# A hand-ordered decoder layer: own instruction lists for the first steps, a ramp and the end, moments of x in groups, and h transposed as 32-bit words

## The reference

```python
def _layernorm(x, eps=1e-05):                       # mean and variance over the last axis
    return (x - m) / jnp.sqrt(v + eps)

x = x + self_attention(_layernorm(x))               # 16 heads of 8
    # attn = softmax(q k^T * 8**-0.5 + (rel_pe @ w_rel)[q - k]); out = attn v @ w_out + b_out
x = x + cross_attention(_layernorm(x), ctx, ctx, mask)
    # 16 heads of 8, scores = where(mask == 0, -1e9, scores)
x = x + ffn(_layernorm(x))                          # 128 -> 512 -> 128
    # act_quant: scale = 127 / max|x| of the row; round(x * scale) / scale
    # weights: round(w / mean|w|) clipped to -1, 0, 1, times mean|w|
    # gate = silu(q(x) @ w_gate); up = q(x) @ w_up; q(gate * up) @ w_down
```

## Time and profile before

| what | value |
|---|---|
| three runs | 458.35, 461.51, 463.34 us, median 461.51 |
| span of the profiled execution, first to last instruction | 457.5 us |
| busy over the span | PE 398.0 (87%), DVE 385.7 (84%), ACT 359.9 (79%), POOL 329.2 (72%) |

### The profile page before, as it was taken

One profiled execution on the slowest core, in us unless ns is written; L12 is line 12 of the kernel. 1 busy time (PEld: TensorE's weight loads), 2 busy tenths in 40 slices (PEclk: granted clock), 3 DMA queues, 4 the chain that ended last, 5 costly groups with the idle time before them and its releaser, 6 DMA issues. The chain is left out here.

```text
span 457.5 us, 18022 instructions
## 1 busy us (share of the span) xinstructions
PE 398.0 (87%) x5405; PEld 311.5 (68%) x5436; DVE 385.7 (84%) x1920; ACT 359.9 (79%) x962; POOL 329.2 (72%) x917
## 2 busy tenths in 40 slices
PE   3267879999999999999999999999999999877762
PEld 2245657777777777777877777778877777654430
DVE  4645467999999999999999999999999999888532
ACT  2214758899999999999999999999999998865542
POOL 6834667888888888888888888888888765654120
PEclk9998999999999999999999999999999999998655
DMA  6654577756666766676657675676567662422100
GB/s 190 162 146 100 140 188 184 173 149 172 173 159 160 191 163 168 150 195 172 170 148 196 175 175 153 164 181 170 152 158 189 165 164 80 101 78 77 30 6 13
DMA packets 100181, 67.27 MB, mean 147 GB/s; under 512 B 73269, under 2 KB 90421, under 8 KB 100085
## 3 DMA queue, kind: packets, MB, share of 16 engines
q1 hardware_dynamic: 98209, 64.08, 54.7%
q10 hardware_dynamic: 1876, 2.03, 1.5%
HBM read 46.08 MB, written 19.07 MB: 142 GB/s over the span
## 5 line engine op out<-in xcount | busy, mean ns | idle before, releaser
L895 DVE CUSTOM_DVE_ANT_0 biased<-bank,mask_bias 128x128 bf16<-128x128 f32 x512 | 112.8, 285 | 4.0 <-PE bank L1128 3.9
L900 DVE TENSOR_REDUCE neg_max_S<-bank 128x4 f32<-128x512 f32 x128 | 85.4, 675 | 21.1 <-PE bank L1128 20.4
L599 ACT ACTIVATE probs_S<-bank 128x512 f32<-128x512 f32 x128 | 72.7, 597 | 11.0 <-PE bank L1148 11.0
L599 ACT ACTIVATE probs_X<-bank 128x512 f32<-128x512 f32 x128 | 72.5, 590 | 7.0 <-PE bank L1148 6.4
L1128 PE MATMUL bank<-stack_k_S,stack_q_S 120*128 120x128 bf16 x512 | 50.5, 223 | 11.7 <-DMA stack_k_S<-scratch_S 11.0
L1148 PEld LDWEIGHTS bank<-stack_q_X,stack_k_X 74*128 74x128 bf16 x512 | 41.1, 100 | 16.6 <-issue 2.1
L1128 PEld LDWEIGHTS bank<-stack_k_S,stack_q_S 120*128 120x128 bf16 x512 | 38.6, 102 | 20.1 <-issue 11.9
L1148 PE MATMUL bank<-stack_q_X,stack_k_X 74*128 74x128 bf16 x512 | 51.4, 224 | 0.0
L1145 PE MATMUL bank<-ident_bf,mask_bias 128*128 128x512 bf16 x128 | 50.6, 396 | 0.0
L1128 PE MATMUL bank<-stack_k_X,stack_q_X 72*128 72x128 bf16 x512 | 45.3, 221 | 2.9 <-DMA stack_k_X<-scratch_X 1.7
L1166 PE MATMUL bank<-probs_X,v_aug_X 128*32 128x128 f32 x1024 | 42.4, 285 | 0.0
(11 more groups left out here) (165 smaller groups left out, 1178.6 us busy)
## 6 DMA issues: line engine op xcount, KB each, us to landing
stack_q_S<-scratch_S SPq DMA_DIRECT2D x32, 288.0 KB
stack_k_S<-scratch_S SPq DMA_DIRECT2D x32, 288.0 KB
stack_q_X<-scratch_X SPq DMA_DIRECT2D x32, 288.0 KB
stack_k_X<-scratch_X SPq DMA_DIRECT2D x32, 288.0 KB
scratch_S<-qk_parts_S SPq DMA_DIRECT2D x32, 192.0 KB, 2.7
scratch_X<-qk_parts_X SPq DMA_DIRECT2D x32, 192.0 KB, 2.7
scratch_S<-qk_parts_S SPq DMA_DIRECT2D x32, 64.0 KB, 1.7
ctxT<-ctx SPq DMA_DIRECT2D x8, 256.0 KB, 4.7
```

Of the source, the lines that this page charges most:

```text
L599: act.activation(probs[a][:, c, :], bank_b[c % 2][:, :], ACT.Exp).then_inc(sems["exp_" + a], 1)
L895: last = dve.tensor_tensor_reduce(biased[:, c, hh, :], quarter(bank_a[c % 2], hh), mask_bias[:, b % 2, :], -1.0, -2.0 * BIG, ALU.add, ALU.min,
L900: dve.tensor_reduce(neg_max[a][:, first_head(c):first_head(c) + 2 * HC - 1:2], bank_a[c % 2][:, :].rearrange("i (h j) -> i h j", h=HC), AX ...
```

## The change

- Every engine has four lists in place of one: `fill` for s = −1 to 3 (S alone), `ramp` for six steps, `step` for the middle and `drain` for the end. An operation now works on every batch that is due by its lag and not yet done (`due`), so a lag in a list that ends a phase can be any large number. The middle lists are close to those of before, though not the same: on DVE the order of X's maxima, the attention sums, the gate and the residual of S is another, and on PE two pieces of X's `attend` stand ahead of `y_transposed`.
- The statistics of x for S are taken in groups (batches 0, 1 to 3, then fours), two steps ahead, with one variance, one mean and one power instruction per group on POOL (128x4). By the third ramp step all are done. The loads of x that feed them go out one per step from s = −1.
- ACT copies the four transpositions of h as 256 words of 32 bits (`hT`, f16, without a bias). The 1536 that thus stays in hT is taken off by a fifth product in `down` with a constant row of −1536 and the column sums of `w_down`. `yT` and `h_q` get their bias as an immediate number.
- `probs` has two buffers for each of S and X. The waits for PSUM banks are worked out from the order (`take`).
- At the start: the stacks' rows of ones go out ahead of the relative parts; ACT's `rel_rows` stand behind part2 of batch 1; `shift_rows` and `weight_sums` run in the first step.

```diff
-STEPS = [(t, t) for t in range(-1, B + 10)]
+LEAD, RAMP, TAIL, LAGS = 4, 6, 5, 12
+MOMENTS = (0, 1, 4, 8, 12, 16, 20, 24, 28, 32)
...
-        def run(step):
-            for s, x in STEPS:
-                step(Step(s, x))
+        def run(begun, fill, ramp, step, drain):
+            for s in range(-1, LEAD):
+                fill(Step(s, None, begun))
+            for x in range(RAMP):
+                ramp(Step(x + LEAD, x, begun))
+            for x in range(RAMP, B + TAIL - LEAD):
+                step(Step(x + LEAD, x, begun))
+            for x in range(B + TAIL - LEAD, B + TAIL + LAGS):
+                drain(Step(x + LEAD, x, begun))
...
+            def load_x(st, lag):
+                for g in st.due("S", lag, "load_x", n=B // GROUP - 2):
+                    batches = slice(X_FIRST[2] + g * GROUP, X_FIRST[2] + (g + 1) * GROUP)
+                    sp.dma_start(x_all[:, batches, :], xs[:, batches, :]).then_inc(sems[f"x_loaded{g}"], 16)
...
+            def fill(st):
+                load_x(st, -1)
+                if st.at(1):
+                    rel_copies(sp)
+                if st.at(0):
+                    rel_rows(sp, stack_q)
+                stack_in("S", st, 0)
+                max_in("S", st, 1)
+                load_c(st, -1)
+                parts_again("S", st, -1)
+                parts_out("S", st, -1)
...
+            def pow_group(st, lag):
+                for g in st.due("S", lag, "pow_group", n=len(MOMENTS) - 1):
+                    lo, hi = MOMENTS[g:g + 2]
+                    pool.wait_ge(sems["veps_S"], g + 1)
+                    pool.tensor_tensor(rstd_s[:, lo:hi], veps_s[:, lo:hi], minus_half[:, 0:hi - lo], ALU.pow)\
+                        .then_inc(sems["rstd_S"], 1)
...
-                act.activation(hT[:].rearrange("p c s -> p (c s)"), bank_t[:, 0:256].bitcast(F16), ACT.Identity,
-                               bias=minus_round16[:, 0:1]).then_inc(sems["hT"], 1)
+                    copy(hT[:].rearrange("p c s -> p (c s)").bitcast(F32), bank_t[:, 0:256]).then_inc(sems["hT"], 1)
...
+                    act.activation(yT[:], half_words.bitcast(F16), ACT.Copy, bias=-ROUND16)\
+                        .then_inc(sems["yT"], 1)
...
+                    act.activation(h_q[:], h[:], ACT.Copy, bias=ROUND16, scale=h_scale[:, 0:1])\
+                        .then_inc(sems["h_q"], 1)
...
+            def ln_group(st, lag):
+                for g in st.due("S", lag, "ln_group", n=len(MOMENTS) - 1):
+                    lo, hi = MOMENTS[g:g + 2]
+                    if lo:
+                        dve.wait_ge(sems["mv_S"], lo)
+                    for b in range(lo, hi):
+                        if b < X_FIRST[2]:
+                            dve.wait_ge(sems[f"x_loaded_first{int(b >= X_FIRST[1])}"], 16)
+                        else:
+                            dve.wait_ge(sems[f"x_loaded{(b - X_FIRST[2]) // GROUP}"], 16)
+                        dve.bn_stats(stats_s[:, b - lo, :], x_all[:, b, :]).then_inc(sems["stats_S"], 1)
+                    for b in range(lo, hi):
+                        dve.wait_ge(sems["stats_S"], b + 1)
+                        dve.bn_aggr(mv_s[:, b, :], stats_s[:, b - lo, :]).then_inc(sems["mv_S"], 1)
...
             def step(st):
+                ln_group(st, -2)
+                ternary_weights(st, 1)
+                attend_sums("S", st, 4)
+                attend_norm("S", st, 4)
+                row_max("X", st, 3, 1)
+                row_max("X", st, 3, 2)
+                row_max("X", st, 3, 3)
+                row_max("S", st, 2, 0)
+                gate(st, 5)
+                residual("S", st, 4)
+                gated(st, 5)
...
+                residual_ffn(st, 5)
+                row_max("X", st, 2, 0)
+                y_max(st, 4)
+                y_unit(st, 4)
+                y_inverse(st, 4)
...
+                    for c in range(CH):
+                        pe.matmul(bank_t[:, 256:384], hT[:, c, :], w_down16[:, c * 128:(c + 1) * 128],
+                                  start=c == 0, stop=False)
+                    last = pe.matmul(bank_t[:, 256:384], minus_offset[:], w_down_sum[:], start=False, stop=True)
+                    last.then_inc(sems["down"], 1)
...
+                on_transposed("S", st, 3)
+                attend("X", st, 3, 0)
+                attend("X", st, 3, 1)
+                y_transposed(st, 4)
+                scores_a("X", st, 2, 3)
```

## The result

The changed kernel is slower: 472.32 us (median of four, 470.38 to 474.09) against 460.31 for the kernel before (four, 458.35 to 463.34), a ratio of 1.0268 [1.0227, 1.0309]. I had forecast 453 with 438 to 464, and gave slower 0.14. The profiled execution took 474.09 with a span of 472.3.

The account below looks back on a forecast made before the run. DVE was taken to bound the middle, by a little. Start 114, 23 steps of 11.5 and an end of 71.5 summed to a span of 450.0 us, median forecast 453, range 438 to 464.

Parts of the forecast that it names:

- I take a period of 11.5: Middle step: DVE's work plus a wait of about 0.1 for tanh gives 11.5 us, −7.1 us over 23 steps.
- first rival: Middle: the gate's wait for tanh sets the period, about 12.3 us, median 471; chance 0.13.
- the third: Rival: lists differ, pairs and waits eat the 0.32, the middle's period stays 11.8, median 460; chance 0.13.
- Moments of x in groups: Middle, DVE: S's statistics of x leave the step, −0.32 us per step, −7.4 us over 23.
- the pairs: Middle, DVE: adjacent dependent instructions, about as many as before, priced at ±0.15 us per step, taken as −0.05.
- Drain: End, after y_inv(25): interleaved lists, shorter hT and S's lead give 71.5 us, −8.2.
- Fill: Start: S alone for five steps, X(0) normalised at 53.5, y_inv(2) at 114 us, +7.8.
- second rival: Start: the x loads delay the stacks and nothing else changes, median 462; chance 0.12.
- ACT: ACT's copies: hT −0.31, yT −0.1, h_q −0.1 us per step, worth nothing in the middle.

Follow-up runs that it names:

- the first experiment: The changed kernel with one line moved: in POOL's middle list max_lo of X stands right behind max_hi of X; 463.81 us, ratio 1.0081.
- the three further orders: Changed kernel with max_lo moved up, plus: y_max behind S's attention sums, 1.0278; or add_shift of S later, 1.0126; or that and yT before part2, 1.0216.

## Why the prediction was wrong

- **The step that failed is "I take a period of 11.5".** It took DVE's work per step and added the wait of one chain that I had checked, y_inv to gate. The work came out as taken (11.00 against 11.07, which is 11.44 less the 0.37 of idle time); DVE's idle time is 1.07 per step in place of some 0.4, most of it waits at other instructions. The loop DVE, POOL, PE, DVE, POOL, DVE of 12.0 could have been read from the new lists with durations of the trace; the first experiment shows that it was the one that held the step at 12.0, and not at the 11.83 where the next wait stands. My first rival had the right kind, a wait that sets the period, at the wrong place; the third, that the lists differ and the gain is eaten by waits, is nearest to what came, though it stopped at 11.8.
- **"Moments of x in groups" was mis-sized, and so were the pairs.** Predicted −0.32 and −0.05 of DVE's work; measured −0.19 for the groups (that run has the change's other edits too, but for the lists) and −0.25 for the order. The step got less of the −0.19: 11.74 against 11.82 with h as words alone. The starts say as much: y_max to y_step was 0.40 with stats_S between and is 0.32 without; the residual to stats_X was 0.33 with mv_S between and is 0.32. That is 0.08 and 0.01 per step, where I took 0.20 and 0.12, the gaps between starts, for the cost of stats_S and mv_S. The two instructions had mostly filled time in which the next, which needs the one before, didn't start anyway. And the −0.25 of the order never reached the step: DVE's idle time grew by more.
- **"Drain" failed on the lead.** I counted S's lead as a saving of part of a step and the own list as interleaving: −8.2. It was −1.5 by that cut. X trails S by a batch more, a price of 10.7 at the end and 6.3 net where nothing else was changed; and the own list gives a microsecond by the profiles. What ACT's shorter copies give at the end isn't shown: it was 1.3 shorter with them in one run and no shorter in the other.
- **"Fill"** was nearly right in its sum (116.6 for 114). X(0) was normalised at 46.9, not 53.5, and from there to y_inv(2) were 69.7, not 60.5. The extra step that I gave to xn_X comes on PE instead: POOL makes xn_X behind S(0)'s residual (44.78), with no step between, and PE transposes it at 52.37, from where y_inv(2) is 64.3 away (60.9 before). The stacks' order (+1.5 for 1) and the loads of x, hidden, came as taken, so the second rival falls. That cover is not free: where the groups stand in the old list, DVE waits 25.2 us for x.
- **"ACT"** was right in all three durations and in their worth of nothing in the middle. The Trainium skill (ScalarE: Activation LUTs, What ACT_TABLE_LOAD costs) gave as estimates 399 for hT and 706 for h_q; the trace has 382 and 715 and agrees within 5%. What I left out were the fifth product's column sums, 1.26 us of DVE at the start; what they cost by their place isn't clear of the clock.

Of the 14.8 us, one line of order takes back 5.3 where it can act, 2.8 went with an earlier start of that execution, and the 6.7 by which that run's span still exceeds the one before have the size and the shape of one more batch of trailing. That the trailing is all of it is argued from that likeness, not shown: a version with the new order and the old trailing wasn't tried. Open are also which loop holds the step at 11.8 to 11.9 in the three further orders, and what makes one execution's start up to 2.8 us longer than another's that does the same.

## What to carry to other kernels

In a hand-ordered pipeline an engine's work per step is only a lower bound: before a reorder is priced, follow each engine's list around until a path closes on itself through in-order neighbours, add its starts, and take the longest such loop, not the one chain that was tight before. An operation that other engines wait for should stand right behind the one it belongs to; three foreign operations between two halves of one result cost 0.2 us of every step here, 4.5 over 23 steps. And count how many batches lie between a pipeline's first and last part: each one more is paid at the end.

## What the runs showed of the hardware

The same number of DVE instructions, 1312, took 258.64 us in one order and 252.91 in another. A small instruction that needs the result of the one before starts 0.32 us after it (y_step behind y_max), one that doesn't need it starts 0.20 after it (stats_S at 259.55, y_max at 259.35), so what a small independent instruction cost between two dependent ones is 0.01 to 0.08 here. The Trainium skill (VectorE: DVE Perf Modes, Rules for kernel authors) says to minimise the count of DVE operations since each one's drain comes regardless; here, in busy time, the order of an equal count was worth more, 0.25 per step, than two instructions less, 0.19, so the measurement goes beyond the rule. No run shows a step that is shorter by either in full. Thirty-two products of `attend` took 1.94 us in a stretch with a granted clock of 0.57, and 1.08 us in one with 1.00; in the 6 us before these stretches PE was busy 4.03 and 4.67 us.
